# Splitting attention output and x1 in rows and turning them by DMA in the second half of a decoder layer

## The reference

```python
x = _layernorm(x + _L0_attn_ref(x, ...))                   # 16 heads, relative positions
x = _layernorm(x + _L0_xattn_ref(ctx_2048, x, mask, ...))  # 8 heads over a context of 512 x 1024 per batch
x = _layernorm(x + _L0_ffn_ref(x, ...))                    # 512 -> 2048 -> 512, fp8 rounding
```

```python
tgt_trans = jnp.einsum('btf,of->bto', tgt, W_tgt) + b_tgt
tgt_update = jnp.einsum('bhts,bshd->bthd', attn, v).reshape(b, t, OUT_SIZE)
cat_tgt = jnp.concatenate([tgt, tgt_update], axis=2)
return jnp.einsum('btf,of->bto', cat_tgt, W_out) + b_out
```

## Time and profile before

| | us |
|---|---|
| median of 3 runs | 1963.22 (1960.47 to 1964.9) |
| profiled execution | 1961.34 |
| its span, first to last instruction | 1959.5 |
| TensorE busy | 1845.5 (94%) |
| VectorE busy | 1333.6 (68%) |
| ScalarE busy | 787.2 (40%) |
| GpSimd busy | 522.3 (27%) |

### The profile page before, as it was taken

One profiled execution on the slowest core, in us unless ns is written; L12 is line 12 of the kernel. 1 busy time (PEld: TensorE's weight loads), 2 busy tenths in 40 slices (PEclk: granted clock), 3 DMA queues, 4 the chain that ended last, 5 costly groups with the idle time before them and its releaser, 6 DMA issues. The chain is left out here.

```text
span 1959.5 us, 33372 instructions
## 1 busy us (share of the span) xinstructions
PE 1845.5 (94%) x12588; PEld 1016.1 (52%) x12588; DVE 1333.6 (68%) x1698; ACT 787.2 (40%) x1209; POOL 522.3 (27%) x546
## 2 busy tenths in 40 slices
PE   5999999999989999868999999999999999999988
PEld 4565555645544665445545455455454554544543
DVE  3588999899879989767565564655655556556521
ACT  3422222222222222247465363562653644626522
POOL 1334864585448326600000001001001000010010
PEclk8999999999999999989999999999999999999999
DMA  6545347425643456565313304104123041041000
GB/s 227 113 119 116 81 116 167 118 71 140 146 108 80 126 141 154 149 141 178 73 42 58 100 1 103 55 1 109 48 46 99 14 103 55 1 104 33 12 33 22
DMA packets 290831, 176.60 MB, mean 90 GB/s; under 512 B 194793, under 2 KB 248041, under 8 KB 290690
## 3 DMA queue, kind: packets, MB, share of 16 engines
q1 hardware_dynamic: 286320, 174.17, 35.6%
q10 hardware_dynamic: 4370, 0.34, 0.2%
HBM read 94.75 MB, written 33.55 MB: 65 GB/s over the span
## 5 line engine op out<-in xcount | busy, mean ns | idle before, releaser
L1362 DVE TENSOR_TENSOR p_lo<-k,p_hi 128x1024 f16<-128x1024 f32 x128 | 156.8, 1225 | 193.8 <-ACT p_hi L1250 193.8
L81 POOL TENSOR_TENSOR vsb<-mvb,consts 128x1 f32<-128x1 f32 x64 | 12.1, 189 | 1029.4 <-DVE mvb L1377 1029.4
L1051 PE MATMUL b_ff<-x2T_hi,w1T_hi 128*128 128x512 f16 x512 | 195.0, 381 | 2.3 <-DVE x2T_lo L1362 2.3
L1407 DVE CUSTOM_DVE_ANT_0 junk<-b_sx,mneg 128x512 f16<-128x512 f32 x256 | 176.1, 688 | 30.6 <-issue 22.2
L1051 PE MATMUL b_ff<-x2T_lo,w1T_hi 128*128 128x512 f16 x512 | 195.0, 381 | 0.0
L1051 PE MATMUL b_ff<-x2T_hi,w1T_lo 128*128 128x512 f16 x512 | 194.8, 380 | 0.0
L1282 ACT ACTIVATE k<-b_st,mbias 128x512 f32<-128x512 f32 x256 | 161.8, 685 | 14.1 <-PE b_st L1095 14.1
L1250 ACT ACTIVATE p_hi<-k 128x1024 f16<-128x1024 f32 x128 | 135.3, 1057 | 44.1 <-PE b_av L1110 41.7
L745 DVE TENSOR_TENSOR prod<-q,k 128x4096 f32<-128x4096 f32 x32 | 143.2, 4476 | 13.0 <-ACT q L677 12.1
L1274 ACT ACTIVATE hq<-b_ff,b 128x512 fp8e4<-128x512 f32 x128 | 88.0, 687 | 155.9 <-PE b_ff L1051 149.2
L595 PE MATMUL pj_b<-winT_hi,xT_hi 128*128 128x512 f16 x384 | 146.3, 381 | 3.9 <-DMA xT_lo<-rows_lo 3.9
(11 more groups left out here) (258 smaller groups left out, 4332.6 us busy)
## 6 DMA issues: line engine op xcount, KB each, us to landing
cn<-in_ctx_dram SPq DMA_DIRECT2D x64, 256.0 KB, 3.1
k<-kT_scratch SPq DMA_DIRECT2D x24, 512.0 KB, 7.8
xn<-in_x_dram SPq DMA_DIRECT2D x32, 256.0 KB, 3.0
x<-in_x_dram SPq DMA_DIRECT2D x32, 256.0 KB, 3.2
x_scratch<-x SPq DMA_DIRECT2D x32, 256.0 KB, 2.2
q<-x_scratch SPq DMA_DIRECT2D x8, 1024.0 KB, 5.6
q<-x_scratch SPq DMA_DIRECT2D x32, 256.0 KB, 4.1
out_dram<-q SPq DMA_DIRECT2D x32, 256.0 KB, 4.3
```

The costliest lines, as they stand in the source:

```text
L1051: mm = pe.matmul(out, a, c, start=(start and n == 0), stop=end)
L1362: dve.tensor_tensor(dst, bank, hi, ALU.subtract).then_inc(out, 1)
L1407: dve.tensor_tensor_reduce(junk[:, :], sx_b[tt % 2][:, :], mneg[:, :], 1.0, NEG, ALU.add, ALU.max, mx[:, h % 2, tt:tt + 1]).then_inc(s["sx ...
```

## The change

Both pairs of halves are made from rows and turned by DMA. TensorE's transposes of x1 and `o`, and the evictions by ScalarE and VectorE, go. In their place, for each of the four tiles: ScalarE copies the float32 rows to f16 (`row_hi`, one buffer per tile, shared by `o` and x1), GpSimd subtracts (the low half lies in place, over the float32 rows), and SyncE issues two transposes, of the high and the low half, into `oT` or `x1T`. `x1T` has one buffer, so x1 of the next batch is turned only once `output_x1` has read that tile (`x1_used`), and `row_hi` passes from `o` to x1 when the output's turn has landed.

`load_heads` is split: the keys keep their place, the values go behind x1's turns. The order on SyncE's queue in the loop becomes: queries, x1 load, mask and keys, then store 0, turn output 0, store 1, turn output 1 to 3, residual loads 0 and 1, stores 2 and 3, turn x1 0 and 1, residual 2, turn x1 2, residual 3, turn x1 3, values. At the start of the half, x1 of batch 0 is turned before SyncE's first load.

```diff
@@ sync
+            def turn_output(b, tt):
+                sp.wait_ge(s["o_row_lo"], 4 * b + tt + 1)
+                stand_alone(sp, alone["sp"])
+                for dst, rows in ((oT[0], row_hi[tt][:, :]), (oT[1], o_lo[tt])):
+                    sp.dma_start_transpose(col(dst, tt), rows).then_inc(o_turned[tt], 16)
+
+            def turn_x1(b, tt, first=False):
+                sp.wait_ge(s["x1_row_lo"], 4 * b + tt + 1)
+                stand_alone(sp, alone["sp"])
+                if not first:
+                    sp.wait_ge(s["x1_used"], 4 * (b - 1) + tt + 1)
+                    stand_alone(sp, alone["sp"])
+                for dst, rows in ((x1T[0], row_hi[tt][:, :]), (x1T[1], x1_lo[tt])):
+                    sp.dma_start_transpose(col(dst, tt), rows).then_inc(x1_turned[tt], 16)
...
+            for tt in range(4):
+                turn_x1(0, tt, True)
             all_stored(sp, w)
-            load_heads(0, True)
+            load_keys(0, True)
+            load_values(0, True)
...
-            load_heads(1, False)
+            load_keys(1, False)
+            for tt in range(4):
+                turn_output(0, tt)
+            for tt in range(4):
+                turn_x1(1, tt)
+            load_values(1, False)
             with sp.Fori(0, NBATCH - 2) as b:
                 for g in range(len(GROUPS)):
                     queries(b + 1, g)
                 load_x1(b + 2)
-                load_heads(b + 2, False)
+                load_keys(b + 2, False)
                 for tt in range(4):
+                    if tt < 2:
+                        store(b, tt)
+                    turn_output(b + 1, tt)
+                for tt in range(2):
+                    load_residual(b + 1, tt, False)
+                for tt in range(2, 4):
                     store(b, tt)
                 for tt in range(4):
-                    load_residual(b + 1, tt, False)
+                    turn_x1(b + 2, tt)
+                    if tt in (1, 2):
+                        load_residual(b + 1, tt + 1, False)
+                load_values(b + 2, False)
@@ gpsimd
+            def x1_rows_lo(b, tt):
+                pool.wait_ge(s["x1_row_hi"], 4 * b + tt + 1)
+                stand_alone(pool, alone["act"])
+                pool.tensor_tensor(x1_lo[tt], x1n[:, tt, :], row_hi[tt][:, :], ALU.subtract).then_inc(s["x1_row_lo"], 1)
...
+            with pool.Fori(0, NBATCH - 2) as b:
+                for tt in range(4):
+                    norm_factors("l2", b, tt)
+                for tt in range(2):
+                    norm_factors("l3", b, tt)
+                output_lo(b + 1, 0)
+                output_lo(b + 1, 1)
+                for tt in range(2, 4):
+                    output_lo(b + 1, tt)
+                    norm_factors("l3", b, tt)
+                for tt in range(4):
+                    x1_rows_lo(b + 2, tt)
@@ tensor
-                    pe.wait_ge(s["xt_lo"], 4 * b + 4)
+                    for tt in range(4):
+                        pe.wait_ge(x1_turned[tt], 32 * (b + 1))
+                        stand_alone(pe, alone["pe"])
...
-                pe.wait_ge(s["o_norm"], 8 * b + 8)
-                for tt in range(4):
-                    transposes(tq_b[tt], o[:, tt, :], s["ot_filled"])
...
-                pe.wait_ge(s["ot_lo"], 4 * b + 4)
                 for tt in range(4):
+                    pe.wait_ge(o_turned[tt], 32 * (b + 1))
+                    stand_alone(pe, alone["pe"])
...
-                x1_transposes(b + 1, False)
                 output_rest(b)
@@ scalar
+            def x1_hi(b, first=False):
...
+                    act.activation(row_hi[tt][:, :], x1n[:, tt, :], ACT.Copy).then_inc(s["x1_row_hi"], 1)
+
+            def output_hi(b):
+
+                act.wait_ge(s["o_norm"], 8 * b + 8)
+                stand_alone(act, alone["act"])
+                for tt in range(4):
+                    act.wait_ge(x1_turned[tt], 32 * (b + 1))
+                    stand_alone(act, alone["act"])
+                    act.activation(row_hi[tt][:, :], o[:, tt, :], ACT.Copy).then_inc(s["o_row_hi"], 1)
...
             for n, (_, high, _) in enumerate(jobs):
+                if n == 2:
+                    x1_hi(0, True)
                 hi(high, bank4(om_b[n % 4]), s["wq_filled"], n + 1, s["wq_hi"], WS)
```

More of the change, by code:

```diff
@@ L887, in phase_b @@
     f16o = [sb(f"f16o{i}", [P, E], F16) for i in range(2)]
+    row_hi = [sb(f"row_hi{i}", [P, E], F16) for i in range(4)]
+    o_lo, x1_lo = ([z[:, tt, :].bitcast(F16)[:, 0:E] for tt in range(4)] for z in (o, x1n))
     stats = [sb(f"statsb{i}", [P, 6], F32) for i in range(4)]
@@ L910, in phase_b @@
     xr_ld = [sem(f"B_xr_ld{i}") for i in range(4)]
+    o_turned, x1_turned = ([sem(f"B_{n}_turned{i}") for i in range(4)] for n in ("o", "x1"))
     out_st = [sem(f"B_out_st{i}") for i in range(4)]
@@ L942, in load_heads, with load_values @@
                 sp.dma_start(k2[0:D2, :, :], k_in[b, 0]).then_inc(s["k_ld"], 16)
+            def load_values(b, first):
                 if first:
@@ L1018, in _ @@
             for tt in range(4):
+                if tt < 2:
+                    store(last - 1, tt)
+                turn_output(last, tt)
+            for tt in range(2):
+                load_residual(last, tt, False)
+            for tt in range(2, 4):
                 store(last - 1, tt)
-            for tt in range(4):
+            for tt in range(2, 4):
                 load_residual(last, tt, False)
@@ L1032, in _, with norm_factors @@
             pool.memset(rows_b[:, :], 0.0).then_inc(s["made"], 1)
[L1033 to L1038, removed]
+            def norm_factors(l, b, tt):
+                pool.wait_ge(s[l + "_mv"], 4 * b + tt + 1)
+                i = tt + (4 if l == "l3" else 0)
+                layer_norm_factors(pool, w, mv[i], vs, rstd[i], s[l + "_rstd"], 4 * (4 * b + tt))
@@ new lines, in _ @@
+            for tt in range(4):
+                x1_rows_lo(0, tt)
+            for tt in range(4):
+                output_lo(0, tt)
+            for tt in range(4):
+                x1_rows_lo(1, tt)
+            with pool.Fori(0, NBATCH - 2) as b:
+                for tt in range(4):
+                    norm_factors("l2", b, tt)
+                for tt in range(2):
+                    norm_factors("l3", b, tt)
+                output_lo(b + 1, 0)
+                output_lo(b + 1, 1)
+                for tt in range(2, 4):
+                    output_lo(b + 1, tt)
+                    norm_factors("l3", b, tt)
+                for tt in range(4):
+                    x1_rows_lo(b + 2, tt)
@@ new lines, in _ @@
+            last = NBATCH - 1
+            for tt in range(4):
+                norm_factors("l2", last - 1, tt)
+            for tt in range(2):
+                norm_factors("l3", last - 1, tt)
+            output_lo(last, 0)
+            output_lo(last, 1)
+            for tt in range(2, 4):
+                output_lo(last, tt)
+                norm_factors("l3", last - 1, tt)
+            for l in ("l2", "l3"):
+                for tt in range(4):
+                    norm_factors(l, last, tt)
@@ L1045, in transposes, with products @@
                 mm.then_inc(done, 1)
-            def products(out, operands, bias, done, start=True):
+            def products(out, operands, bias, done, start=True, stop=True):
                 for n, (a, c) in enumerate(operands):
-                    end = bias is None and done is not None and n == len(operands) - 1
+                    end = stop and bias is None and done is not None and n == len(operands) - 1
                     mm = pe.matmul(out, a, c, start=(start and n == 0), stop=end)
@@ L1289, in exponentials_high @@
                 hi(ph[0][:, part, :], pf[:, part, :], s["st_exp"], 32 * b + 4 * h + 2 * half + 2, s["p_hi"])
[L1291 to L1293 removed]
+            def x1_hi(b, first=False):
+                if first:
+                    for i in range(3):
+                        act.wait_ge(w.x1_out[i], 16 * len(range(i, NB * T, 3)))
+                act.wait_ge(w.x_ld, 16 * (b + 1))
+                stand_alone(act, alone["act"])
+                for tt in range(4):
+                    if not first:
+                        act.wait_ge(o_turned[tt], 32 * b)
+                        stand_alone(act, alone["act"])
+                    act.activation(row_hi[tt][:, :], x1n[:, tt, :], ACT.Copy).then_inc(s["x1_row_hi"], 1)
+            def output_hi(b):
+                act.wait_ge(s["o_norm"], 8 * b + 8)
+                stand_alone(act, alone["act"])
+                for tt in range(4):
+                    act.wait_ge(x1_turned[tt], 32 * (b + 1))
+                    stand_alone(act, alone["act"])
+                    act.activation(row_hi[tt][:, :], o[:, tt, :], ACT.Copy).then_inc(s["o_row_hi"], 1)
             def queries_hi(b, i):
@@ L1313, in heads @@
                     normalize("l3", ff, 1)
-                for tt in range(4):
```

(2 more changed lines are left out.)

24 lines of the change are left out of this document (9 added, 15 removed).

## The result

The changed kernel takes 2008.0 us in the median (2006.19 to 2009.78, 4 runs), the kernel before 1961.85 in the same measurement: a ratio of 1.024 (1.021 to 1.027). The forecast was 1979 us with a range of 1961 to 1996, so the direction came out and the size did not: +46 us instead of +17.

A forecast was written before the change was run, and what follows sets the result against it. It took TensorE to bound the second half's loop and transfers its start; six turns -1, first turn +9.5, start +10.5 and end -1.75 sum to +17 us, forecast 1979 us, range 1961 to 1996.

The forecast's parts named there:

- the turn inside the loop: Six loop turns: 3.5 us of transposes saved, a 2.5 us wait, 0.85 for clock; about -0.2 us each.
- The chain: SyncE's queue in a loop turn: transposes 19.7 us, plain DMAs 3.8, waits 1.8; 25.3 us, from 1071.4 to 1096.7.
- The first turn: Batch 0 to 1, nothing hides the transposes: +8.9 us and about 0.6 for clock, taken as 9.5 (6 to 12).
- The clock: TensorE behind its loop wait: half level for 3.4 us costs 1.7, taken for every other turn, 0.85 a turn.
- The bounds: Loop turn: wait near 0 and 3.5 us gained, to wait 5 and 1.5 lost; six turns -21 to +15.
- The start: Start of the second half: x1's turns delay SyncE's loads, first scores at 878 instead of 867.34, +10.5 us (5 to 13).
- The end: After the last turn, which only loses its output transposes on TensorE: -1.75 us.
- (a): Loop turns: SyncE's chain is short enough, no wait, -21 us in six; sum -6 us, 1956; chance 0.1.
- The sharper form: SyncE's queue: a transpose holds it no longer than a plain copy, 0.5 us; sum -19 us, 1943; chance 0.03.
- (b): Batch 0: its own gaps absorb the start's 10.5 us shift; sum +7 us, 1970; chance 0.12.
- (c): Loop turns: query copies queue behind the late value loads, 4 us more each; sum +41 us, 2002; chance 0.08.
- (d): Loop and start: a shorter chain and part of the start absorbed, ending within 4 us of before; chance 0.1.

The follow-up runs named there:

- e_residual_late: The changed kernel with the last two residual loads of a turn moved from between x1's turns to behind them; 1993.4 us, ratio 1.015 to the kernel before.
- e_warm: The changed kernel plus 24 useless TensorE products a turn between the output products and the wait for x1; 1989.0 us, ratio 1.013 to the kernel before.
- e_values_first: The changed kernel with the loop's value loads put back behind the key loads, ahead of all turns; 2035.6 us, ratio 1.037 to the kernel before.
- e_stage_x0pe: As e_stage, but x1 of batch 0 is transposed on TensorE and SyncE's start order is that of the kernel before; 1937.7 us.
- e_stage: The changed kernel with the next batch's x1 turned during the heads into the query tiles, then brought to x1T by two plain copies; 1949.6 us.
- e_x1_only: The kernel before with only x1 split in rows and turned by DMA, the output still transposed on TensorE; 1969.2 us, ratio 1.003.

## Why the prediction was wrong

**The step that failed** is the turn inside the loop: "It waits 2.5 us", -0.2 us with the clock. The wait was 5.9, and a turn lost 4.1 us: 24.5 us in six instead of a gain of 1, 25 of the 30 us between forecast and measurement. The mechanism was named, TensorE behind SyncE's queue; sizes in it were off. Of the 4.3 us between -0.2 and +4.1 the chain makes 2.8 and the clock 1.5; a third item lengthened the wait and not the turn.
- *The chain.* SyncE started where I put it (1071.4 + 23.03 = 1094.43; row 1094.46) and the last transpose landed 2.5 us after its issue, as forecast; TensorE started 0.1 later (1123.92 - 1121.29 = 2.6). In between it took 28.1 us, not 25.3. From the timeline: 16 transposes 20.74 us instead of 19.7, one of them stretched to 2.21; seven plain DMAs 3.95 instead of 3.8; the rest, hand-overs, 3.4 us instead of a dozen at 0.15. I had that 0.15 from a row of four plain loads, and it does hold among transposes alone. The first turn has the same 16 in one chain without a plain DMA between them, and took 21.1 us where 21.5 were forecast (rows below). In the loop the hand-overs with a plain DMA on one side or on both took 0.25 to 0.35 us, all but one, and 2.4 of the 3.4 us together. e_residual_late confirms the price at its margin: two plain loads less, 1.28 us less.
- *TensorE asked earlier.* The pause of 0.71 us at the loop's head shrank to 0.16. Where a wait exists, what TensorE gains ahead of it is lost in it, so this made the wait 0.55 us longer and the turn no longer.
- *The clock.* I took 1.7 us for every other turn, 0.85. From 1123.92 to 1129.77 stand 14 products in 5.85 us that take 3.0 at the full clock (0.215 from one to the next): 2.8 us lost in this turn; e_warm measured 2.4 as the mean of six. My price from the earlier trace rows was that of one wait of 3.4 us, behind which the half level ended after 3.4; behind the waits of 4.9 to 6.2 us here it lasted 3.0 to 5.9. It doesn't simply grow with the wait: behind those of 8.1 to 9.6 us in e_values_first it lasted 2.5 to 5.5.

The first turn's chain, its first and its last transpose:

```profile
966.18 1.26 SPq L939 DMA_TRANSPOSE oT_hi<-row_hi  x1
...
986.04 1.27 SPq L948 DMA_TRANSPOSE x1T_lo<-q  x1
```

**The bounds** of that step were a wait of 5 us and, in six turns, +15. The wait, at 5.9, left them a little: I let the hand-overs double or GpSimd stretch, not the transposes as well. The rest of the way to +24.5 is the clock: +15 in six turns is 2.5 a turn, which beside the loss of 1.5 leaves it 1.0, about a half-level stretch of 1.7 us every other turn.

**What held.** The start: SyncE's mask at 856.80 (forecast 856.8), first scores at 878.50 (878), +11.2 us (10.5); e_stage_x0pe gives it back. That the scores came out to 0.3 us is luck: the query copies went out 2.0 us earlier than forecast (872.38, not 874.4), and the first low half took 4.8 us to land where I had 2. x1 itself landed at 857.8; the forecast's 857.6 is a slip of 0.3, its own terms give 857.9. The first turn: +10.2 us (9.5), in two waits, 6.90 and 4.20, where I had one. 9.1 of it is the chain (8.9 forecast); the other 1.1 stands ahead of the turn, where the output was whole 85.4 us behind the first scores instead of 84.3, and the 0.6 for the clock falls behind the queries, in the next turn. That start and first turn would add, and that SyncE's queue is the narrow place, were the right reading.

The end came out +1.4 instead of -1.75: the last turn's half level lies there. In e_warm it is -1.8.

**The rivals.** (a) needed the chain to be short; it was longer. The sharper form, a transpose that holds SyncE no longer than a copy, is refuted by line 948 of the change (x1's transposes: ns min/median/max, first to last us):

```profile
L948 SPq DMA_TRANSPOSE x1T_hi<-row_hi x32: 1188/1195/1232, 846.3 to 1799.2; - x32
L948 SPq DMA_TRANSPOSE x1T_lo<-q x32: 1253/1260/1456, 847.5 to 1800.4; - x32
```

e_stage's plain copies of four times as much took 0.55 and 0.61 us of SyncE. "Advanced Engine Details and Errata" of the Trainium skill (X-Bar Transpose) has transpose DMAs as fast as regular ones. In landing the runs don't speak against it (2.5 us, and 2.9 to 5.3 for e_stage's larger copies), though none compares like with like; in issue a transpose holds SyncE twice as long, and the measurement decides. (b), (c) and (d) didn't happen: batch 0 absorbed nothing, and the query copies went out behind the value loads without delay. GpSimd's subtractions stayed at 1.16 us in the median; of VectorE's 32 instructions with two inputs one in each turn, seven in all, took 1.51 us instead of 0.69 (none did before), at 1093.41 beside three such subtractions, off TensorE's path. That agrees with "GPSIMD Engine Reference" of the Trainium skill (Specifications), and no run here shows that it cost time.

## What to carry to other kernels

Moving work from a bound engine to a DMA queue costs the queue's serial issue time, which is a sum over every instruction between the first and the last, and it is worth doing where the queue has time before the data is asked for: the same 16 transposes a turn lost 4.1 us in one chain and gained 4.15 when half of them went out during the heads. Price such a chain by rows with the same neighbours, and add to a long wait of TensorE the half clock behind it: waits of 4.9 to 6.2 us cost 2.4 more here, while behind e_x1_only's, of 1.0 to 1.8 us in the loop, no half level shows. At a start that is bound by transfers, as this one is, put nothing ahead of the loads.

## What was not expected of the hardware

The issue of one and the same load isn't constant: four value loads held SyncE for 3.03 us behind the turns, 7.72 directly behind the key loads, and 9.45 at the start of the second half. In five of the six turns one output transpose, the fourth tile's first, took 2.0 to 2.2 us instead of 1.2; what held it was not tried and stays open.
